# Delta rule: the inverse of each block of 14 by two blocks of 7 and one product of halves

## The chip, the cores and the metric

One core of a Trainium2 chip. The time is device microseconds (us) of one execution. The kernel before took 1900.37 us, the median of 3 runs (1899.91 to 1904.96).

## The reference, cut to what matters

A decoder of two layers for 16 sequences of 112 tokens, width 256. The diff touches the first mixer, a gated delta rule with 8 heads of 128:

```python
def step(S, inp):
    q_t, k_t, v_t, beta_t, alpha_t = inp
    S = S * alpha_t[..., None, None]
    kv = jnp.einsum('bhk,bhkv->bhv', k_t, S)
    S = S + jnp.einsum('bhk,bhv->bhkv', k_t, (v_t - kv) * beta_t[..., None])
    o_t = jnp.einsum('bhk,bhkv->bhv', q_t, S)
    return (S, o_t)
_, o = lax.scan(step, S0, (qt, kt, vt, bt, at))
```

Then a norm and a gate of o, an output product, cross attention, experts, attention, cross attention and a feed-forward part. Over all 112 tokens the recurrence is a triangular system, 112x112 for each sequence and head, which the kernel inverts in blocks: 14x14 blocks on the diagonal, pairs of them joined to 28x28, and the rest by products on TensorE.

## The kernel before, in words

**Units.** A unit is one head and four sequences (NG = 4 units to a head, 32 units). Each engine has its program written out in one order and waits on semaphores. In the main loop (lines 1022 to 1052 for DVE), unit u is solved and put out while the keys of unit u + 8 are projected. A head's inverse is made in the four units before its first solve. `head_due(u, left)` gives the head that is due in `left` units, so the units fall in four kinds by u mod 4:
- kind 0: rows 1 to 9 of the due head's blocks (`rows(h4, ...)`, in three places of the unit)
- kind 1: rows 10 and 11 ahead of the unit's key taps, rows 12 and 13 and the copy `rows_first` further on (`h3`). On SP, `exchange` stores both forms of the inverse and reads them back as pairs
- kind 2: the join of the pairs in four parts (`h2`): products 0 and 2 on POOL, sums 1 and 3 on DVE; sum 3 is the last step of DVE's unit. On SP, `joined` stores the result, as the last step of the unit
- kind 3: `spread` (SP) puts it into the big tile, ahead of the unit's `diagonal`, which stores the diagonal blocks of a new unit; `gather` reads a head's blocks into `NI`.

Head 0 is done ahead of the loop: there all 13 rows run in one piece, while PE does the first keys. Head 7 falls into the last eight units, which have a loop of their own.

**A row.** All 128 blocks of 14x14 of a head (16 sequences, 8 blocks) lie on 128 partitions, 196 values each. Row t is a product of t x t elements (L507) and a sum (L509), each waiting for the one before: row t of `NI` times the t x t corner of the inverse, summed.

**DVE's order in a unit**: key taps (L914, three instructions), the gate of unit u - 1 (`tail` 3, L976), L964, query taps, the output added to x (`tail` 5, L983), L968, then rows or the first sum of the join, the key matrix (L934), value taps (L914), rows, the z gate (L950), the query matrix (L940), L958, and rows or the second sum. Row work stands in this queue like the rest.

**PE's order in a unit** around it: key projection (L556), L645, query projection (L556), L679, L651, L589, then `tail` 4: L686, the output product, which waits for `gated` from DVE's L976. PE's transposes of the values (L616) wait for the value taps. Every period that is spoken of below runs from one L686 to the next.

**ACT and POOL.** ACT scales the output (L836), which waits for POOL's root (L1117 and L1119), and starts each tap sum (L790, L793, L804). POOL makes the masks of decay (L1092, L1104, L1112, L1113) and the products of the join (L528).

Of the kernel before, what the change touches and what calls it, by code (L numbers as in the profile page):

```python
# [12 lines left out]
ALU = mybir.AluOpType  # L13
# [72 lines left out]
def memory(nc, ctx):  # L86
# [74 lines left out]
    k.R = [p3(k.big_a[0:T, 6, :]), p3(k.big_b[0:T, 7, :])]  # L161
    at = 2 * G * DK + G * FAR
    k.A, k.A_less = four(spare[:, at:at + G * MID]), four(spare[:, at + G * MID:at + G * FAR])
    k.NI, k.TI = (k.big_a[:, 0, n * BLOCK * BLOCK:(n + 1) * BLOCK * BLOCK] for n in range(2))
    k.tri_tmp = k.big_a[:, 7, :]
    later = k.expert_w[:, :, :].rearrange("p a b -> p (a b)")
    k.Dn = [later[0:T, n * B * T:(n + 1) * B * T].rearrange("p (s t) -> p s t", s=B) for n in range(2)]
# [302 lines left out]
def is_late(u):  # L470

    return u >= UNITS - AHEAD

# [18 lines left out]
    return k.kT[n], k.qT[n]  # L492


def invert_row(dve, k, s, h, t):

    first = (2 * (BLOCK - 1) + 1) * h + 2 * (t - 1)
    if t == 1:
        dve.wait_ge(s["ni_in"], 32 * (h + 1))
        if h:  # L500
            dve.wait_ge(s["td_w"], 32 * h)
    if first:
        dve.wait_ge(s["tri"], first)
    NI = k.NI.rearrange("p (m t) -> p t m", m=BLOCK)[:, t, 0:t]
    TI = k.TI.rearrange("p (c m) -> p c m", c=BLOCK)
    tmp = k.tri_tmp[:, 0:t * t].rearrange("p (c m) -> p c m", c=t)
    dve.tensor_tensor(tmp, NI.unsqueeze(1).to_broadcast([128, t, t]), TI[:, 0:t, 0:t], ALU.mult).then_inc(s["tri"], 1)  # L507
    dve.wait_ge(s["tri"], first + 1)
    dve.tensor_reduce(TI[:, 0:t, t], tmp, AXX, ALU.add).then_inc(s["tri"], 1)  # L509


def rows_first(dve, k, s, h):

    dve.wait_ge(s["tri"], (2 * (BLOCK - 1) + 1) * (h + 1) - 1)
    dve.tensor_copy(k.TIn.rearrange("p (t c) -> p t c", t=BLOCK),
                    k.TI.rearrange("p (c t) -> p t c", c=BLOCK)).then_inc(s["tri"], 1)
# [390 lines left out]
def gdn_dve(dve, k, s):  # L907
# [77 lines left out]

    def rows(h, ts):
        for t in ts:
            invert_row(dve, k, s, h, t)

    start_dve_stats(dve, k, s, 0)  # L990
    for g in range(1, NG):
# [8 lines left out]
    for a in range(1, AHEAD + 1):  # L1000
        for slot in (2, 4, 3, 10):
            if a == 1 and slot == 10:
                start_dve_gate_in(dve, k, s, 1)
            elif a == 2 and slot == 2:
                start_dve_gate_out(dve, k, s, 1)
            elif a == NG + 1 and slot == 3:
                rows(0, range(1, BLOCK))
                rows_first(dve, k, s, 0)
            elif a == NG + 3 and slot == 4:
                for part in (1, 2, 3):  # L1010
                    join(dve, k, s, 0, part)
            elif a == NG + 4 and slot == 4:
                values(0, 7)
            if slot in (4, 10):
                keys(a - 1, slot)
            elif a < AHEAD:
                keys(a, slot)
        if a == 2:
            dve.tensor_scalar(k.norm_w[:, :], k.norm_w[:, :], 0.5, None, ALU.mult).then_inc(s["setup_dve"], 1)
    values(0, 9)  # L1020
    solve(0, "M")
    for u in range(UNITS - AHEAD):
        a = u + AHEAD
        h4, h3, h2 = head_due(u, 4), head_due(u, 3), head_due(u, 2)
        if h3 is not None:
            rows(h3, (10, 11))
        keys(a, 2)
        if u:
            tail(u - 1, 3)
        solve(u, "less")  # L1030
        keys(a, 3)
        if u:
            tail(u - 1, 5)
        solve(u, "R")
        if h4 is not None:
            rows(h4, (1, 2, 3, 4))
        if h3 is not None:
            rows(h3, (12, 13))
            rows_first(dve, k, s, h3)
        if h2 is not None:  # L1040
            join(dve, k, s, h2, 1)
        keys(a, 4)
        values(u + 1, 7)
        if h4 is not None:
            rows(h4, (5, 6))
        values(u + 1, 9)
        keys(a, 10)
        solve(u + 1, "M")
        if h4 is not None:
            rows(h4, (7, 8, 9))  # L1050
        if h2 is not None:
            join(dve, k, s, h2, 3)
    for u in range(UNITS - AHEAD, UNITS):
        more = is_unit(u + 1)
        h4, h3, h2 = head_due(u, 4), head_due(u, 3), head_due(u, 2)
        if h4 is not None:
            rows(h4, range(1, 6))
        if h3 is not None:
            rows(h3, range(11, BLOCK))
            rows_first(dve, k, s, h3)  # L1060
        if h2 is not None:
            join(dve, k, s, h2, 1)
        tail(u - 1, 3)
        solve(u, "less")
        if more:
            values(u + 1, 7)
            values(u + 1, 9)
            solve(u + 1, "M")
        else:
            cross_head_dve(dve, k, s, 0, 0)  # L1070
        solve(u, "R")
        if h4 is not None:
            rows(h4, range(6, 11))
        if h2 is not None:
            join(dve, k, s, h2, 3)
        tail(u - 1, 5)
# [90 lines left out]
def gdn_sp(sp, k, s, a):  # L1167
# [25 lines left out]
    def gather(h):  # L1193

        sp.wait_ge(s[f"nd_w{h % 2}"], 256 * (h // 2 + 1))
        if h:
            sp.wait_ge(s["tri"], (2 * (BLOCK - 1) + 1) * h)
            sp.wait_ge(s["pair"], 4 * h)
        for e, at in enumerate((FIRST, SECOND)):
            sp.dma_start(square(half(k.NI, e)), pairs(k.nd[h % 2, :, :, at, at])).then_inc(s["ni_in"], 16)  # L1200
        for e in range(2):
            sp.dma_start(square(half(k.C_full, e)), pairs(k.nd[h % 2, :, :, FIRST, SECOND])).then_inc(s["c_in"], 16)

    def exchange(h):


        sp.wait_ge(s["tri"], (2 * (BLOCK - 1) + 1) * (h + 1))
        if h >= 2:
            sp.wait_ge(s[f"dn_in{h % 2}"], 192 * (h // 2))
        for dram, tile in ((k.td, k.TI), (k.tn, k.TIn)):  # L1210
            sp.dma_start(dram[h % 2].rearrange("e s p a b -> (e s p) (a b)"), tile).then_inc(s["td_w"], 16)
        sp.wait_ge(s["td_w"], 32 * (h + 1))
        if h:
# [28 lines left out]
    for u in range(-AHEAD, UNITS):  # L1242
# [2 lines left out]
            joined(0)  # L1245
        h = head_due(u, 1) if u >= 0 else 0 if unit == NG + 3 else None
        if h is not None:
            spread(h)
        if is_unit(unit):
            if unit % NG == 0 and 1 <= unit // NG < HEADS - 1:  # L1250
# [1523 lines left out]
def sync_program(sp, k, s, a, out):  # L2774
# [170 lines left out]
```

## Time and profile before

| what | value |
|---|---|
| median of 3 runs | 1900.37 us |
| the profiled execution, its own time | 1900.15 us |
| its span | 1898.8 us |
| mean granted clock of TensorE | 0.994 |
| busy: PE, DVE, ACT, POOL | 96%, 63%, 38%, 37% |
| delta-rule stage | from the start to some 575 us |
| rows of head 0 | 61.6 to 70.0 us |
| main loop, 24 units | some 103 to 480 us |

The profile lists the instructions of each engine by line, with the time for which the engine stood idle just before them and what ended that. PE is busy nearly all of the time, so what matters in the delta-rule stage is where PE stood idle and for whom. A busy time of PE is not PE at its peak: matmuls are pipelined and their ends are modelled.

### The profile page before, as it was taken

How to read it: one execution, taken by the hardware profiler on the slowest of the kernel's cores; microseconds unless marked ns; L12 is line 12 of the kernel's file. 1: busy time of each engine (PE TensorE's matmuls, PEld its weight loads, DVE VectorE, ACT ScalarE, POOL GpSimd, SP SyncE). 2: the span in 40 equal slices, each digit the busy share in tenths (PEclk: the TensorE clock that was granted, in tenths of full speed). 3: DMA queues.
4: the chain of work that ended last, by engine and by line, in shares of the span. 5: the costliest groups of instructions: out<-in, count | busy, mean ns of one | idle time of the engine just before them, and what ended most of it. 6: DMA issues, size and time to landing. Idle time of an engine off the chain costs nothing.

```text
span 1898.8 us, 40078 instructions
## 1 busy us (share of the span) xinstructions
PE 1828.3 (96%) x15048; PEld 1324.9 (70%) x15048; DVE 1196.1 (63%) x3307; ACT 712.7 (38%) x1883; POOL 705.9 (37%) x758
## 2 busy tenths in 40 slices
PE   7799999999889999999999999999999999999999
PEld 4467777777666666666445766666659979889698
DVE  6878788778646767767766666667665334234332
ACT  4233434343435555554001465655632212122221
POOL 4644544454215766665000267666634000000000
PEclk9899999999999999999999999999999999999999
DMA  6111111111103100100000001001040000000000
GB/s 188 29 23 21 32 17 29 21 25 16 23 13 125 37 26 26 37 26 20 1 1 1 10 20 29 20 20 30 11 178 1 1 11 1 10 1 1 10 1 10
DMA packets 94591, 52.22 MB, mean 28 GB/s; under 512 B 77256, under 2 KB 86336, under 8 KB 93632
## 3 DMA queue, kind: packets, MB, share of 16 engines
q1 hardware_dynamic: 94400, 49.65, 9.8%
q8 instruction: 122, 2.00, 0.4%
q14 instruction: 69, 0.57, 0.1%
HBM read 44.18 MB, written 5.45 MB: 26 GB/s over the span
## 4 chain that ended last, share of the span: by engine, by line
PE 75%; DVE 11%; issue 6%; POOL 4%; ACT 2%; SPq 1%; DMA 1%; DVEq 0%; ACTq 0%; POOLq 0%
PE ps L2536 18%; PE ps L1519 6%; PE ps L2408 5%; PE ps L1541 5%; PE ps L2067 5%; PE ps L1596 4%; PE ps L1557 4%; PE ps L1575 4%; PE ps L556 3%; PE ps L2614 3%; DVE big_b L914 3%; PE ps L686 2%; DVE big_a L507 2%; PE ps L1528 2%; PE ps L1662 2%
## 5 line engine op out<-in xcount | busy, mean ns | idle before, releaser
L1980 POOL TENSOR_TENSOR h_w<-h_w 125x336 int32<-125x336 int32 x384 | 336.3, 906 | 210.6 <-ACT h_w L1761 210.4
L1865 DVE CUSTOM_DVE_ANT_0 h_w<-ps,h_w 112x375 f32<-112x375 f32 x512 | 263.1, 543 | 0.5 <-PE ps L1519 0.2
L914 DVE SCALAR_TENSOR_TENSOR big_b<-ps,taps,big_b 128x444 f32<-128x444 f32 (+2 forms) x288 | 193.9, 673 | 67.7 <-ACT big_b L790 49.6
L1761 ACT ACTIVATE h_w<-ps 125x336 f32<-125x336 f32 x512 | 198.0, 468 | 21.6 <-PE ps L1541 21.6
L272 POOL TENSOR_TENSOR rstd<-var_eps,minus_half 112x4 f32<-112x4 f32 x12 | 12.2, 1018 | 406.5 <-DVE var_eps L259 406.5
L1541 PEld LDWEIGHTS ps<-h_w 32*125 32x125 f32 x3072 | 96.0, 183 | 62.0 <-issue 61.2
L1541 PE MATMUL ps<-h_w 32*125 32x112 f32 x3072 | 118.0, 282 | 7.7 <-DVE h_w L1865 5.0
L1874 DVE TENSOR_TENSOR h_w<-h_w,ps 128x112 f32<-128x112 f32 x128 | 34.7, 271 | 141.7 <-PE ps L1528 141.5
L1519 PE MATMUL ps<-h_w 32*112 32x375 f32 x1024 | 121.2, 519 | 0.8 <-DVE h_w L1865 0.8
L2067 PE MATMUL ps<-expert_w,big_a 128*112 128x512 f32 x256 | 113.6, 595 | 0.0
L556 PE MATMUL ps<-h_w,w 128*128 128x448 f32 x256 | 108.2, 545 | 4.7 <-ACT h_w L812 4.7
L556 PE MATMUL ps<-h_w,kq_w 128*128 128x448 f32 x256 | 111.3, 558 | 0.0
L1557 PE MATMUL ps<-h_w 125*32 125x112 f32 x3072 | 100.8, 263 | 0.5 <-POOL h_w L1980 0.4
L2408 PE MATMUL ps<-xT,w 128*128 128x448 f32 x256 | 97.7, 540 | 1.1 <-DVE big_a L2423 1.1
L2178 DVE SCALAR_TENSOR_TENSOR x<-ps,small,x 112x256 f32<-112x256 f32 x128 | 61.9, 483 | 37.0 <-PE ps L2067 34.0
L2067 PEld LDWEIGHTS ps<-expert_w,big_a 128*112 128x112 f32 x256 | 43.9, 177 | 57.5 <-issue 48.0
L1884 DVE TENSOR_TENSOR h_w<-h_w 125x336 f32<-125x336 f32 x128 | 81.7, 638 | 2.5 <-ACT h_w L1761 2.4
L2408 PEld LDWEIGHTS ps<-xT,w 128*128 128x128 f32 x256 | 48.3, 190 | 46.6 <-issue 44.8
L1557 PEld LDWEIGHTS ps<-h_w 125*32 125x32 f32 x3072 | 69.9, 109 | 15.6 <-issue 1.2
L1112 POOL TENSOR_TENSOR big_a<-big_a,w 112x448 f32<-112x448 f32 x32 | 31.3, 980 | 131.3 <-ACT big_a L798 112.1
L2536 PE MATMUL ps<-big_b,h_w 128*128 128x224 f32 x384 | 79.0, 353 | 0.0
L2536 PE MATMUL ps<-big_a,h_w 128*128 128x224 f32 x384 | 78.5, 352 | 0.0
(357 smaller groups left out, 3848.4 us busy)
## 6 DMA issues: line engine op xcount, KB each, us to landing
h_w<-in_h SPq DMA_DIRECT2D x2, 4096.0 KB, 16.9
kq_w<-in_ctxT SPq DMA_DIRECT2D x16, 375.0 KB, 3.1
h_w<-in_ctxT SPq DMA_DIRECT2D x16, 375.0 KB, 3.2
h_w<-in_mask SPq DMA_DIRECT2D x16, 164.1 KB, 3.1
kq_w<-in_kq_w SPq DMA_DIRECT2D x8, 256.0 KB, 3.4
w<-in_vz_w SPq DMA_DIRECT2D x8, 256.0 KB, 3.5
blocks<-h_w SPq DMA_DIRECT2D x128, 12.2 KB
expert_w<-in_expert_w SPq DMA_DIRECT2D x1, 2048.0 KB
```

The lines of the kernel that those rows point to most:

```text
L556: ins = pe.matmul(ps[:, bank, 0:GT], w[:, c, :], c_in[:, c, :], start=(c == 0), stop=(c == KD - 1))
L914: dve.scalar_tensor_tensor(p3(dst)[:, :, i:], p3(ps[:, bank, 0:GT])[:, :, 0:T - i], k.taps[:, h, n, TAPS - 1 - i:TAPS - i], p3(dst)[:, :, ...
L1519: pe.matmul(ps[0:T, score_bank(Q, r), 0:S2], k.Qz[n % 2][rows, z, m, :], k.Kx[n % 2][rows, z, m, :], start=True, stop=True).then_inc(s["S" ...
L1541: ins = pe.matmul(ps[0:CK, turned_bank(Q, r), c * T:(c + 1) * T], k.Kx[n % 2][rows, z, m, c * CK:(c + 1) * CK], k.Qx[Q % 2][rows, :], star ...
L1557: ins = pe.matmul(ps[32 * r:32 * r + 32, 6, q * T:(q + 1) * T], k.Vx[n % 2][:, c, 4 * q + r, :], k.PTx[(4 * Q + r) % RING][:, c * T:(c + 1 ...
L1761: act.activation(k.PTx[(4 * Q + r) % RING], ps[0:CK, turned_bank(Q, r), 0:NC * T], ACT.Exp).then_inc(s["exp"], 1)
L1865: dve.tensor_tensor_reduce(k.masked[r % 2], ps[0:T, score_bank(Q, r), 0:S2], k.mask_add[n % 2], -1.0, 3.0e38, ALU.add, ALU.min, k.neg_max[ ...
L1884: dve.tensor_tensor(P, P, k.mask_I[n % 2], ALU.min).then_inc(s["weights0"], 1)
L1980: pool.tensor_tensor(P.bitcast(I32), P.bitcast(I32), k.mask_I[n % 2], ALU.mult).then_inc(s["weights"], 1)
L2067: ins = pe.matmul(ps[0:T, bank, :], k.moe_xT[g % 2][:, c, j * T:(j + 1) * T], k.expert_w[:, c, e * D:(e + 2) * D], start=(c == 0), stop=(c ...
L2408: ins = pe.matmul(k.ps[:, 2 + 2 * n + m % 2, 0:GT], k.w12[:, n, c, m * 128:(m + 1) * 128], k.xT[:, c, :], start=(c == 0), stop=(c == KD - 1))
L2536: ins = pe.matmul(ps[:, product_bank(p, m), FIRST_HALF], lhsT, rhs, start=(c == 0), stop=(c == QT - 1))
```

## The change

Each 14x14 block is cut in two blocks of 7 on its diagonal and a 7x7 block between them. Rows 1 to 6 of both small blocks are made in the same instructions (`invert_half_row`; row 1 is a copy), then the block between by two products with a sum each (`join_halves`, parts 0 and 1, 343 elements each). Both tiles get a row's width more room so that a view reaches both halves. Where row 7 and further stood, the parts of `join_halves` stand. The second sum of the pairs' join goes from the end of unit kind 2 to the start of the next, and `joined` on SP with it; in the last eight units neither is moved.

```diff
+SMALL_DONE = 2 * HALF + 2
...
-    k.NI, k.TI = (k.big_a[:, 0, n * BLOCK * BLOCK:(n + 1) * BLOCK * BLOCK] for n in range(2))
+    wide = BLOCK * (BLOCK + 1)
+    k.NI, k.TI = (k.big_a[:, 0, n * wide:(n + 1) * wide] for n in range(2))
...
-def invert_row(dve, k, s, h, t):
-
-    first = (2 * (BLOCK - 1) + 1) * h + 2 * (t - 1)
+def halves_of(block):
+
+    return block.rearrange("p (e r) -> p e r", e=2)[:, :, 0:HALF * BLOCK].rearrange("p e (c m) -> p e c m", m=BLOCK)[:, :, :, 0:HALF]
+
+
+def invert_half_row(dve, k, s, h, t):
+
+    first = SMALL_DONE * h + (2 * t - 3 if t > 1 else 0)
+    N, inverse = halves_of(k.NI), halves_of(k.TI)
     if t == 1:
         dve.wait_ge(s["ni_in"], 32 * (h + 1))
         if h:
             dve.wait_ge(s["td_w"], 32 * h)
-    if first:
+            dve.wait_ge(s["tri"], first)
+        dve.tensor_copy(inverse[:, :, 0, 1], N[:, :, 0, 1]).then_inc(s["tri"], 1)
+    else:
         dve.wait_ge(s["tri"], first)
-    NI = k.NI.rearrange("p (m t) -> p t m", m=BLOCK)[:, t, 0:t]
-    TI = k.TI.rearrange("p (c m) -> p c m", c=BLOCK)
-    tmp = k.tri_tmp[:, 0:t * t].rearrange("p (c m) -> p c m", c=t)
-    dve.tensor_tensor(tmp, NI.unsqueeze(1).to_broadcast([128, t, t]), TI[:, 0:t, 0:t], ALU.mult).then_inc(s["tri"], 1)
+        tmp = k.tri_tmp[:, 0:2 * t * t].rearrange("p (e c m) -> p e c m", e=2, c=t)
+        dve.tensor_tensor(tmp, N[:, :, 0:t, t].unsqueeze(2).to_broadcast([128, 2, t, t]), inverse[:, :, 0:t, 0:t],
+                          ALU.mult).then_inc(s["tri"], 1)
+        dve.wait_ge(s["tri"], first + 1)
+        dve.tensor_reduce(inverse[:, :, 0:t, t], tmp, AXX, ALU.add).then_inc(s["tri"], 1)
+
+
+def join_halves(dve, k, s, h, part):
+
+    first = SMALL_DONE * h + 2 * HALF - 3 + 2 * part
+    N = k.NI[:, 0:BLOCK * BLOCK].rearrange("p (m t) -> p t m", m=BLOCK)
+    inverse = k.TI[:, 0:BLOCK * BLOCK].rearrange("p (c m) -> p c m", c=BLOCK)
+    shape = [128, HALF, HALF, HALF]
+    tmp = k.tri_tmp[:, 0:HALF ** 3].rearrange("p (c a b) -> p c a b", c=HALF, a=HALF)
+    between = k.tri_tmp[:, HALF ** 3:HALF ** 3 + HALF * HALF].rearrange("p (c a) -> p c a", c=HALF)
+    if part == 0:
+        rows, cols, to = inverse[:, 0:HALF, 0:HALF], N[:, HALF:, 0:HALF], between
+    else:
+        rows, cols, to = between, inverse[:, HALF:, HALF:].rearrange("p n t -> p t n"), inverse[:, 0:HALF, HALF:]
+    dve.wait_ge(s["tri"], first)
+    dve.tensor_tensor(tmp, rows.unsqueeze(2).to_broadcast(shape), cols.unsqueeze(1).to_broadcast(shape), ALU.mult).then_inc(s["tri"], 1)
     dve.wait_ge(s["tri"], first + 1)
-    dve.tensor_reduce(TI[:, 0:t, t], tmp, AXX, ALU.add).then_inc(s["tri"], 1)
+    dve.tensor_reduce(to, tmp, AXX, ALU.add).then_inc(s["tri"], 1)
...
     def rows(h, ts):
         for t in ts:
-            invert_row(dve, k, s, h, t)
+            if t < HALF:
+                invert_half_row(dve, k, s, h, t)
+            else:
+                join_halves(dve, k, s, h, t - HALF)
...
-                rows(0, range(1, BLOCK))
+                rows(0, range(1, HALF + 2))
                 rows_first(dve, k, s, 0)
...
-        h4, h3, h2 = head_due(u, 4), head_due(u, 3), head_due(u, 2)
+        h4, h3, h2, h1 = head_due(u, 4), head_due(u, 3), head_due(u, 2), head_due(u, 1)
+        if h1:
+            join(dve, k, s, h1, 3)
         if h3 is not None:
-            rows(h3, (10, 11))
+            rows(h3, (7,))
         keys(a, 2)
...
         solve(u, "R")
         if h4 is not None:
-            rows(h4, (1, 2, 3, 4))
+            rows(h4, (1, 2, 3))
         if h3 is not None:
-            rows(h3, (12, 13))
+            rows(h3, (8,))
             rows_first(dve, k, s, h3)
         if h2 is not None:
             join(dve, k, s, h2, 1)
         keys(a, 4)
         values(u + 1, 7)
         if h4 is not None:
-            rows(h4, (5, 6))
+            rows(h4, (4,))
         values(u + 1, 9)
         keys(a, 10)
         solve(u + 1, "M")
         if h4 is not None:
-            rows(h4, (7, 8, 9))
-        if h2 is not None:
-            join(dve, k, s, h2, 3)
+            rows(h4, (5, 6))
     for u in range(UNITS - AHEAD, UNITS):
...
-            rows(h4, range(1, 6))
+            rows(h4, range(1, 4))
         if h3 is not None:
-            rows(h3, range(11, BLOCK))
+            rows(h3, range(7, HALF + 2))
             rows_first(dve, k, s, h3)
...
-            rows(h4, range(6, 11))
+            rows(h4, range(4, 7))
...
         h = head_due(u, 1) if u >= 0 else 0 if unit == NG + 3 else None
         if h is not None:
+            if h and not is_late(u):
+                joined(h)
             spread(h)
...
         h = head_due(u, 2) if u >= 0 else None
-        if h is not None:
+        if h is not None and is_late(u):
             joined(h)
```

The counts of the semaphore `tri` and the DMAs of `NI` and `TI` follow: 16 steps a head where there were 27, and the first 196 values of each wider tile.

## Rows read from the trace of the kernel before

**Rows 1.** The page: busy time, share and instructions of each engine.
```profile
PE 1828.3 (96%) x15048; PEld 1324.9 (70%) x15048; DVE 1196.1 (63%) x3307; ACT 712.7 (38%) x1883; POOL 705.9 (37%) x758
```

**Rows 2.** Busy time by stretch: length, PE, PEld, DVE, ACT, POOL, clock, DMA share, GB/s.
```profile
182.90:246.35 63.45, 61.84 (x416) 45.58 (x416) 52.15 (x102) 25.69 (x80) 29.99 (x31) 1.00 0.14 24
...
373.20:438.30 65.10, 63.52 (x417) 46.49 (x417) 52.27 (x103) 25.68 (x80) 30.02 (x31) 0.97 0.14 20
```

**Rows 3.** Timeline of PE: start, us, line, tiles [idle before, its releaser].
```profile
214.09 1.98 PE L686 MATMUL ps<-gdn_out_w,big_b 128*112 128x256 f32 x8 [0.36 <-DVE big_b L976]
...
229.47 1.89 PE L686 MATMUL ps<-gdn_out_w,big_b 128*112 128x256 f32 x8
...
240.84 0.83 PE L645 MATMUL ps<-big_b,h_w 112*84 112x84 f32 x8
...
246.35 1.98 PE L686 MATMUL ps<-gdn_out_w,big_b 128*112 128x256 f32 x8 [1.23 <-DVE big_b L976]
...
261.72 1.89 PE L686 MATMUL ps<-gdn_out_w,big_b 128*112 128x256 f32 x8
```

**Rows 4.** Timeline of DVE in unit kind 0 and the start of kind 2.
```profile
233.01 0.38 DVE L507 TENSOR_TENSOR big_a<-big_a 128x1 f32<-128x1 f32 x1
...
233.61 0.67 DVE L507 TENSOR_TENSOR big_a<-big_a 128x4 f32<-128x4 f32 x1
...
235.30 0.62 DVE L934 TENSOR_TENSOR h_w<-ps,big_a 112x448 f32<-112x448 f32 x1
...
237.85 0.78 DVE L507 TENSOR_TENSOR big_a<-big_a 128x25 f32<-128x25 f32 x1
...
239.23 0.61 DVE L950 SCALAR_TENSOR_TENSOR big_b<-big_b,ps 128x448 f32<-128x448 f32 x1
...
240.71 0.22 DVE L507 TENSOR_TENSOR big_a<-big_a 128x49 f32<-128x49 f32 x1
...
243.62 2.09 DVE L914 SCALAR_TENSOR_TENSOR big_b<-ps,taps,big_b 128x444 f32<-128x444 f32 x3
...
258.56 2.10 DVE L914 SCALAR_TENSOR_TENSOR big_b<-ps,taps,big_b 128x444 f32<-128x444 f32 x3 [2.61 <-ACT big_b L790]
```

**Rows 5.** Groups of DVE by shape: count, busy us, mean ns of one, idle before.
```profile
L507 DVE TENSOR_TENSOR big_a<-big_a 128x169 f32<-128x169 f32 x8 | 3.6, 447 | 0.3
...
L509 DVE TENSOR_REDUCE big_a<-big_a 128x13 f32<-128x169 f32 x8 | 2.6, 330 | 0.3
...
L528 DVE TENSOR_TENSOR w<-w 128x1372 f32<-128x1372 f32 x1 | 2.0, 1957 | 0.0
...
L507 DVE TENSOR_TENSOR big_a<-big_a 128x49 f32<-128x49 f32 x8 | 1.8, 230 | 0.1
```

**Rows 6.** Timeline of POOL in unit kind 0.
```profile
233.33 0.94 POOL L1104 TENSOR_TENSOR big_a<-upto,small 112x448 f32<-112x448 f32 x1
...
236.64 1.04 POOL L1119 TENSOR_TENSOR rstd<-var_eps,minus_half 112x4 f32<-112x4 f32 x1
237.65 0.94 POOL L1092 TENSOR_TENSOR soft<-before,small 112x448 f32<-112x448 f32 x1
```

**Rows 7.** Head 0: DVE's row 4 and copy, PE behind them, busy time by stretch.
```profile
63.73 0.18 DVE L507 TENSOR_TENSOR big_a<-big_a 128x16 f32<-128x16 f32 x1
...
69.71 0.33 DVE L515 COPY w<-big_a 128x196 f32<-128x196 f32 x1
...
72.10 1.84 PE L594 MATMUL ps<-big_b 128*112 128x112 f32 x8 [5.37 <-DVE big_b L914]
...
72.10:76.40 4.30, 4.30 (x12) 2.98 (x13) 2.95 (x5) 0.55 (x1) 3.65 (x4) 0.50 0.20 42
```

**Rows 8.** Timeline of PE in head 5.
```profile
373.19 3.57 PE L686 MATMUL ps<-gdn_out_w,big_b 128*112 128x256 f32 x8 [1.23 <-DVE big_b L976]
```

**Rows 9.** Head 7: timelines of POOL and PE.
```profile
501.10 2.89 POOL L528 TENSOR_TENSOR w<-w 128x1372 f32<-128x1372 f32 x1 [7.63 <-issue]
...
506.65 0.60 PE L679 MATMUL ps<-ident,xn 112*128 112x112 f32 x4 [0.88 <-ACT xn L836]
```

More of the change, by code:

```diff
@@ L508, in invert_row @@
     dve.wait_ge(s["tri"], first + 1)
-    dve.tensor_reduce(TI[:, 0:t, t], tmp, AXX, ALU.add).then_inc(s["tri"], 1)
+    dve.tensor_reduce(to, tmp, AXX, ALU.add).then_inc(s["tri"], 1)
 def rows_first(dve, k, s, h):
-    dve.wait_ge(s["tri"], (2 * (BLOCK - 1) + 1) * (h + 1) - 1)
+    dve.wait_ge(s["tri"], SMALL_DONE * (h + 1) - 1)
     dve.tensor_copy(k.TIn.rearrange("p (t c) -> p t c", t=BLOCK),
-                    k.TI.rearrange("p (c t) -> p t c", c=BLOCK)).then_inc(s["tri"], 1)
+                    k.TI[:, 0:BLOCK * BLOCK].rearrange("p (c t) -> p t c", c=BLOCK)).then_inc(s["tri"], 1)
@@ L1196, in gather @@
         if h:
-            sp.wait_ge(s["tri"], (2 * (BLOCK - 1) + 1) * h)
+            sp.wait_ge(s["tri"], SMALL_DONE * h)
             sp.wait_ge(s["pair"], 4 * h)
         for e, at in enumerate((FIRST, SECOND)):
-            sp.dma_start(square(half(k.NI, e)), pairs(k.nd[h % 2, :, :, at, at])).then_inc(s["ni_in"], 16)
+            sp.dma_start(square(half(k.NI[:, 0:BLOCK * BLOCK], e)), pairs(k.nd[h % 2, :, :, at, at])).then_inc(s["ni_in"], 16)
         for e in range(2):
@@ L1204, in exchange @@
     def exchange(h):
-        sp.wait_ge(s["tri"], (2 * (BLOCK - 1) + 1) * (h + 1))
+        sp.wait_ge(s["tri"], SMALL_DONE * (h + 1))
         if h >= 2:
             sp.wait_ge(s[f"dn_in{h % 2}"], 192 * (h // 2))
-        for dram, tile in ((k.td, k.TI), (k.tn, k.TIn)):
+        for dram, tile in ((k.td, k.TI[:, 0:BLOCK * BLOCK]), (k.tn, k.TIn)):
             sp.dma_start(dram[h % 2].rearrange("e s p a b -> (e s p) (a b)"), tile).then_inc(s["td_w"], 16)
@@ L2789, in sync_program @@
                        (k.minus_strict[:, :], "minus_strict"), (k.norm_w[:, :], "norm_w"),
-                       (k.off_blocks[:, :], "off_blocks"), (k.TI, "block_eye")):
+                       (k.off_blocks[:, :], "off_blocks"), (k.TI[:, 0:BLOCK * BLOCK], "block_eye")):
         sp.dma_start(tile, a[name]).then_inc(s["c_gdn"], 16)
```

## Prediction

> **What bounds the kernel now.** I read the page first: PE is busy 96% of the span and DVE 63% [rows 1]. That is an average over stages, and the diff touches only the delta-rule stage, so I cut the trace by heads. One head's four units take 63.45 us, of which PE is busy 61.84 [rows 2]: the stage runs at PE's pace, less some idle time. The timeline of PE shows whose it is. The output matmuls of L686 stand once in each unit, in a fixed place of PE's order, so their starts are a clock: 214.09, 229.47, 246.35, 261.72 [rows 3]. Three of a head's four periods are 15.4 to 15.8; that of kind 0 (the unit that does most rows) is 246.35 - 229.47 = 16.88. It holds a 1.23 wait for DVE's L976, a slip of 0.14 at L645 (the 112x84 matmuls start at 240.84 and take 0.83) and a first matmul after idling that makes L686 1.98 instead of 1.89. A period without a stall is 261.72 - 246.35 = 15.37. So DVE costs 16.88 - 15.37 = 1.51 us a head here. The same wait of 1.23 or 1.24 stands ahead of L686 in six heads (units 1, 5, 9, ... 21). A second, smaller one (0.36 at 214.09, kind 3) has another cause: POOL runs both of the join's products in unit kind 2, its root comes late, and ACT's scaling and tap behind it.
>
> In DVE's timeline of that period [rows 4] the reader is to see that DVE does not wait once: rows 1 to 4 from 233.01, rows 5 and 6 from 237.85, rows 7 to 11 from 240.71, and only at 243.62 the key taps, behind which L976 stands. In the next unit, where DVE waits for ACT's tap, they start at 258.56, 3.16 ahead of L686. Without the stall L686 would stand at 229.47 + 15.37 = 244.84, and the taps would be ready at 241.7. The row work is on the path.
>
> **The second sum: nothing.** The join's part 3 was the last thing that DVE did in unit kind 2 and becomes the first in kind 3. Nothing stands between the two places. On SP, `joined` was the last step of kind 2 and now comes just ahead of `spread` in kind 3: again the same order, before the same four diagonal stores. In the last eight units neither moves. Queue for queue the instructions are in the same order, so I cost it at 0; it has one answer.
>
> **The inversion, in instructions.** Before, a head has 13 products, 13 sums and a copy (27 instructions, 819 products of elements). After, it has a copy, 5 pairs over both halves (2t² elements, 180 in all), 2 pairs of 343 elements and the old copy: 16 instructions, 866 elements. The elements stay; 11 instructions go, with some 0.15 us fixed and 0.03 between two.
>
> The prices are from the groups by shape [rows 5]. A product of 49 elements takes 230 ns and one of 169 takes 447, of which 150 is the floor of one element: 1.6 to 1.8 ns an element. The only product of DVE with 98 short rows of operands in a row, 1372 elements, takes 1957: 1.32 ns an element. For 343 that gives 0.60 to 0.75 us. I take 0.75, since its second operand is read with a stride of 14, as in the rows of today. Sums are 330 for 169 elements, 1.04 ns each over a floor of 0.155: 0.51 for 343. A half join is then 0.75 + 0.51 + 0.07 = 1.33. The pairs of both halves come to 0.17 + 0.16, 0.18 + 0.17, 0.20 + 0.19, 0.24 + 0.21 and 0.27 + 0.23 for t = 2 to 6.
>
> The Trainium skill (VectorE: DVE Perf Modes, the section on the TRN2 errata) states (N + 151)/0.96 ns for an fp32 tensor_tensor. An estimate from that page is 515 ns for N = 343; it also gives 333 for N = 169 where the trace has 447, so the trace decides. With the page's price a half join would be 0.24 cheaper and the sum below about 0.5 us larger.
>
> **Contention between DVE and POOL.** Two products take far longer than their shape: 4 elements, 0.67, from 233.61, and 25 elements, 0.78, from 237.85 [rows 4]. They end at 234.28 and 238.63, just as POOL's L1104 (233.33 + 0.94) and L1092 (237.65 + 0.94) end [rows 6]. A DVE product with both inputs in SBUF stands while POOL runs such an operation; sums do not. The Trainium skill (SBUF — State Buffer, the section that has the exclusive lock of the shared port pair) says the same and adds that the one that starts first holds it for its whole instruction. By that rule a product that comes ahead of POOL's operation is free and one just behind waits it out, which makes this term two-valued here.
>
> **Walk through kind 0 of a head.** Row 1 and the products of row 2 still stand behind POOL until 234.28. Then the sum of row 2 and row 3 end at 234.9 instead of 235.30: 0.4 gained (0.8 if the copy slips through). L934 and the three value taps take 2.55, so row 4 comes at 237.43. There POOL's root (L1119, 236.64 + 1.04) is running, not yet L1092. Bounds: the product gets in between the two, at 237.7, and the pair ends at 237.95; or it stands until 238.6 and ends at 238.85. L950 started at 239.23, so DVE is then 1.38 or 0.46 ahead. Its last stretch took 243.62 - 240.71 = 2.91. Now it is rows 5 and 6 (0.24 + 0.21 + 0.27 + 0.23 + 0.14 = 1.09) and half a join (1.29), 2.4 with rounding: 0.5 gained. The key taps start 1.9 or 1.0 earlier than 243.62, at 241.7 or 242.6. PE can reach L686 at 244.84 and starts it 2.73 after those taps start (246.35 - 243.62): they must start by 242.1. So the stall is gone, or 0.5 of it is left. The gain per head is 1.5 or 1.0. I take 1.4, nearer to the first since row 4 meets the boundary between two POOL operations, where the product at 233.01 was let through. What is late next is PE itself; ACT's tap allows 241.7.
>
> Six heads: 6 x 1.4 = 8.4. In unit 0 the value taps are also late for PE's transposes (0.30, L616), and 0.4 earlier they are not: 0.3.
>
> **Kind 1.** Rows 12 and 13 with the copy took 1.87 ahead of L934 at 251.86; half a join and the copy take 1.7. PE does not wait for DVE there now. SP's stores, the exchange and POOL's first product come some 0.3 earlier relative to PE; they gain nothing, since POOL's second product stands behind DVE's sum, and that sum behind L968. So 0, and the 0.36 of kind 3 stays.
>
> **Head 0.** Its rows run in one piece, and PE stands for it (5.37 us before 72.10 [rows 7]). The first three rows again meet POOL and keep their times. From row 4 at 63.73 to the copy at 69.71 it is 5.98; after, rows 4 to 6 take 0.39 + 0.45 + 0.50 + 0.2 = 1.5 and the two half joins 2.7: 4.2. Gain 1.8, all of it on the path, since the exchange, POOL's first product and the taps behind it all shift. After the idle time PE ran at a granted clock of 0.50, its 1.2 GHz level, for 4.3 us [rows 7]; it would now start at 70.3, and I take it that the clock falls all the same, since 3.6 us of idle time are left. Ends: 1.5, and 3.6 if it doesn't fall, as 4.3 us at half speed are some 2 us too many.
>
> **The clock in head 5.** In one of the six stalls L686 took 3.57 instead of 1.98 [rows 8]; the mean granted clock of that head is 0.97 where it is 1.00 in the other, and it took 65.10 [rows 2]. PE had stood idle for 1.23 just before. Without that idle time I expect it to go: 1.6. Ends: 0 and 1.6.
>
> **Head 7**, in the last eight units. DVE mostly waits there, so shorter rows are hidden. One chain counts: rows, exchange, POOL's product at 501.10, which holds POOL's root until 504.07, and PE's L679 waits 0.88 for ACT behind it [rows 9]. The rows end 0.8 earlier; the root is then held by its squares. Gain 0.5 (0.3 to 0.6).
>
> **Sum.** 8.4 + 0.3 + 1.8 + 1.6 + 0.5 = 12.6 us. The profiled execution took 1900.15 (span 1898.8 and 1.35 around it), 0.2 from the median of 1900.37. 1900.15 - 12.6 = 1887.5.
>
> **Rivals.**
> 1. POOL holds the ports. Row 4 stands until 238.6 in each head, and the clock still dips once. 6 x 1.0 + 0.3 + 1.8 + 0.5 = 8.6, 1891.5. For it: 0.67 and 0.78 in the rows. Against: row 4 would come while L1119 runs, ahead of L1092. Chance 0.22.
> 2. The clock gives more. Head 0's matmuls keep or regain full speed, 6 x 1.5 + 0.3 + 3.6 + 1.6 + 0.5 = 15.0, 1885.1. Against: 3.6 us of idle time are three times the 1.23 at which it fell once in six. Chance 0.18.
> 3. The wide products are slow. The stage returns little: with two broadcast operands in four dimensions each costs 1.6 us (4.7 ns an element), the last stretch of kind 0 then takes 3.2, 0.3 more than the 2.91 of today, against 0.46 to 1.38 that row 4 brings. 6 x 0.6 and 0.5 for head 7 are 4.1, 1896. No row is above 1.8 ns on DVE. Chance 0.08.
> 4. Slower. The same mechanism further: if a product of 343 costs more than 1.8 to 2.7 us, the key taps start later than 243.62, PE's wait grows by the excess in each of six heads, and head 0 loses twice the excess. At 3.5 us that is 6 x 1.2 + 3.7 = 11 slower, 1911. It would take over 8 ns an element. Chance 0.04.
>
> That the change does not do what it says holds for its second half, costed at 0, and moves no number.
>
> **How the numbers follow.** The forecast, stall gone, dip gone, head 0 by DVE's time, has 0.48. The range reaches to rivals 1 and 2 and their ends: rival 2 with products of 0.60 is 1884; rival 1 with head 0 at 1.5 and head 7 at 0.3 is 1892.0, which I round up to 1893 since the clock is priced from single events. I give 1883.5 to 1893. A measurement of this kernel tells about 0.3% (5.7 us) from no change. Forecast and rivals 1 and 2 are faster by more: 0.88. Rival 3 is within: 0.08. Rival 4: 0.04.
>
> **What would show it.** After: L686 in the timeline of PE every 15.4 also in kind 0, with a wait for L976 under 0.4; DVE idle before the key taps of kind 1, released by ACT L790; 343-element products of 0.6 to 0.75 and sums of 0.51; row work of head 0 in 6.6 instead of 8.4; the same 0.36 in kind 3; and the join's sum in the same place. What would make it wrong: the wide product's price, where row 4 falls against POOL's L1092, and the clock.

## The result, and the profile after

The kernel with the change takes 1885.78 us (median of 4 runs, 1884.67 to 1886.9); the kernel before takes 1900.14 (1897.98 to 1904.96). The ratio is 0.9921, 95% interval 0.9901 to 0.9941: 0.8% faster, with 1887.5 forecast and a range of 1883.5 to 1893.0. The profiled execution took 1886.9, the slowest of the four, with a span of 1885.5; before it was 1898.8. So the two traces differ by 13.3 us, where the medians differ by 14.4, and it is the 13.3 that have to be found.

The page of after first, then the first head's cut that [rows 2] made of before (length, busy time of PE, PEld, DVE, ACT and POOL, granted clock, DMA share, GB/s):

```profile
PE 1823.0 (97%) x15048; PEld 1324.1 (70%) x15048; DVE 1183.2 (63%) x3219; ACT 712.2 (38%) x1883; POOL 709.5 (38%) x758
...
177.44:239.15 61.71, 61.38 (x418) 45.58 (x417) 50.59 (x91) 25.64 (x80) 30.46 (x30) 1.00 0.15 25
```

DVE has 88 instructions and 12.9 us fewer, 11 a head. The head takes 61.71 where it took 63.45, while PE's busy time in it fell by only 0.46: the rest, 1.28, was PE standing idle. POOL's busy time rose by 3.6 us over the span; it has the same 758 instructions, so some of them take longer. Nearly all of it is the second mask of L1134 in kind 1, which takes 1.46 where it takes 0.93 elsewhere (the mean of its group is 1087 ns for 978), beside DVE's second wide product.

The timeline of PE in the same head (start, length, line, tiles; L713 is what L686 was):

```profile
223.87 1.89 PE L713 MATMUL ps<-gdn_out_w,big_b 128*112 128x256 f32 x8
...
235.11 0.76 PE L672 MATMUL ps<-big_b,h_w 112*84 112x84 f32 x8
...
239.15 1.89 PE L713 MATMUL ps<-gdn_out_w,big_b 128*112 128x256 f32 x8
...
254.43 1.89 PE L713 MATMUL ps<-gdn_out_w,big_b 128*112 128x256 f32 x8
...
270.20 1.98 PE L713 MATMUL ps<-gdn_out_w,big_b 128*112 128x256 f32 x8 [0.33 <-DVE big_b L1003]
```

Against [rows 3]: the period of kind 0 is 239.15 - 223.87 = 15.28, with no wait and no slip at the 112x84 matmuls (0.76 for 0.83); the next is 15.28 too; only the small wait of kind 3 is left (0.33 for 0.36).

The timeline of DVE in that period, which answers to [rows 4], and of POOL, which answers to [rows 6]:

```profile
227.42 0.38 DVE L511 COPY big_a<-big_a 128x2 f32<-128x2 f32 x1
227.83 0.86 DVE L515 TENSOR_TENSOR big_a<-big_a 128x8 f32<-128x8 f32 x1
...
229.31 0.62 DVE L961 TENSOR_TENSOR h_w<-ps,big_a 112x448 f32<-112x448 f32 x1
...
231.86 0.20 DVE L515 TENSOR_TENSOR big_a<-big_a 128x32 f32<-128x32 f32 x1
...
234.75 0.77 DVE L534 TENSOR_TENSOR big_a<-big_a 128x343 f32<-128x343 f32 x1
235.55 0.51 DVE L536 TENSOR_REDUCE big_a<-big_a 128x49 f32<-128x343 f32 x1
235.99 2.10 DVE L941 SCALAR_TENSOR_TENSOR big_b<-ps,taps,big_b 128x444 f32<-128x444 f32 x3
```

```profile
227.73 0.93 POOL L1134 TENSOR_TENSOR big_a<-upto,small 112x448 f32<-112x448 f32 x1
...
231.04 1.04 POOL L1149 TENSOR_TENSOR rstd<-var_eps,minus_half 112x4 f32<-112x4 f32 x1
232.05 0.93 POOL L1122 TENSOR_TENSOR soft<-before,small 112x448 f32<-112x448 f32 x1
```

The key taps start 239.15 - 235.99 = 3.16 ahead of L713; before it was 2.73, which was too little. Row 2's product (8 elements, 0.86) still stands until POOL's L1134 ends, at 228.7. But row 4's product, on which the forecast turned, runs at 231.86 in 0.20, in the last fifth of POOL's root L1149 (231.04 to 232.08) and just ahead of L1122. It is so in five of the six kinds 0. In the first one (unit 0) DVE and POOL stand a little differently, and the product comes just behind the start of L1122 and waits it out:

```profile
108.00 0.93 POOL L1122 TENSOR_TENSOR soft<-before,small 112x448 f32<-112x448 f32 x1
```

```profile
108.14 0.84 DVE L515 TENSOR_TENSOR big_a<-big_a 128x32 f32<-128x32 f32 x1
```

### Where the 13.3 us went

The start of the same output matmuls in the kernel before (those of [rows 3] and [rows 8] are not repeated). Rows with fewer than 8 matmuls come from a narrow window that cut them off; only their starts are read:

```profile
119.50 1.76 PE L686 MATMUL ps<-gdn_out_w,big_b 128*112 128x256 f32 x7 [1.24 <-DVE big_b L976]
182.92 1.33 PE L686 MATMUL ps<-gdn_out_w,big_b 128*112 128x256 f32 x5 [1.24 <-DVE big_b L976]
309.76 1.55 PE L686 MATMUL ps<-gdn_out_w,big_b 128*112 128x256 f32 x6 [1.23 <-DVE big_b L976]
438.24 1.98 PE L686 MATMUL ps<-gdn_out_w,big_b 128*112 128x256 f32 x8 [1.23 <-DVE big_b L976]
```

and in after:

```profile
115.63 1.55 PE L713 MATMUL ps<-gdn_out_w,big_b 128*112 128x256 f32 x6 [0.38 <-DVE big_b L1003]
177.44 1.89 PE L713 MATMUL ps<-gdn_out_w,big_b 128*112 128x256 f32 x8
300.85 1.46 PE L713 MATMUL ps<-gdn_out_w,big_b 128*112 128x256 f32 x6
363.05 1.25 PE L713 MATMUL ps<-gdn_out_w,big_b 128*112 128x256 f32 x5
424.75 1.46 PE L713 MATMUL ps<-gdn_out_w,big_b 128*112 128x256 f32 x6
```

Before minus after is 3.87, 5.48, 7.20 (at 246.35 [rows 3]), 8.91, 10.14 (at 373.19 [rows 8]) and 13.49. From head to head it grows by 1.61, 1.72, 1.71, 1.23 and 3.35: 1.6 to 1.7 for each head's kind 0, with two exceptions. In the head that gained 1.23, after has a longer stall of its own in kind 3 (0.82 at 332.40; POOL's first product of the join came 1.6 later there than in the head before, relative to PE): 0.5 lost. In the head that gained 3.35 the slow clock of [rows 8] is gone: 1.6. Of the first 3.87, 2.16 are there by PE's query projection of unit 0 (100.63 before, 98.47 after), which is head 0; the other 1.71 is unit 0's kind 0: 0.47 up to the transposes, 0.38 at the 112x84 matmuls and 0.86 of the wait, which is 0.38 where it was 1.24. Behind the last of these another 0.1 comes from the period after that stall, next to nothing from head 7 (there a gain and a loss of 0.6 cancel, below), and 0.3 is lost in the rest of the program, which is not touched.

| term | forecast | measured |
|---|---|---|
| kind 0 of unit 0, with its value taps | 1.4 + 0.3 | 1.7 |
| kind 0, the other five | 7.0 | 8.6 |
| head 0 | 1.8 | 2.2 |
| slow clock in head 5 | 1.6 | 1.6 |
| head 7 | 0.5 | 0.0 |
| second sum moved | 0 | 0 (a run of its own, below) |
| later stall at 332.40, rest of the program | 0 | -0.8 |
| sum | 12.6 | 13.3 |

### The profile page after: what moved, and what is told of

It is laid out like the page before. It is cut to its first block, busy times and chain, and to the rows that moved or that the text cites. A ratio compares the mean times of both kernels' runs of the same rounds, so it can differ in the third digit from the quotient of the medians.

```text
span 1885.5 us, 39990 instructions
## 1 busy us (share of the span) xinstructions
PE 1823.0 (97%) x15048; PEld 1324.1 (70%) x15048; DVE 1183.2 (63%) x3219; ACT 712.2 (38%) x1883; POOL 709.5 (38%) x758
## 4 chain that ended last, share of the span: by engine, by line
PE 80%; DVE 7%; issue 6%; POOL 4%; ACT 2%; SPq 1%; DMA 1%; DVEq 0%; ACTq 0%; POOLq 0%
PE ps L2568 18%; PE ps L1551 6%; PE ps L2440 5%; PE ps L1573 5%; PE ps L2099 5%; PE ps L583 5%; PE ps L1628 4%; PE ps L1589 4%; PE ps L1607 4%; PE ps L2646 3%; PE ps L713 2%; PE ps L1560 2%; PE ps L1694 2%; PE ps L1639 1%; DVE big_b L941 1%
```

## The experiments

Theory A is the forecast's: DVE's row work is on the path in kind 0 and head 0, and the time is in the instructions taken out. The rivals that had to be told apart: the moved sum brings part of it (B); the slack is not at kind 0, so that row work anywhere costs the same (C); the clock and not the work sets the size (D). All experiments but one (the root edit on the kernel before) start from the kernel with the change; the times are medians, and each ratio is against the kernel before on the same chip, whose median was 1899.69 to 1901.35 there. So times of different runs are compared to within 1 or 2 us, and finer readings are taken from the traces.

### The inversion alone

```diff
-        if h1:
-            join(dve, k, s, h1, 3)
...
+        if h2 is not None:
+            join(dve, k, s, h2, 3)
```

with `joined` back at the end of SP's unit.

> The changed kernel with the join's second sum and its stores back in their old places in the program. My theory: these places hold the same order on each queue, so the time is that of the changed kernel, 1884.5 to 1887, and the page shows the same waits. Rival: the move carries part of the gain (the sum no longer stands in unit kind 2), and without it the kernel is 2 us or more slower.

Measured: 1885.34 us (1885.17 to 1885.76), ratio 0.9926 (0.9911 to 0.9941), span 1884.4. The move is worth 0.4 us the wrong way, inside the spread of either: B falls, and the term of 0 stands. Its L713 stand 15.28, 15.37 or 15.77 apart just as in after.

### The row work put back, by place

The first sum of a half join (0.51, 0.54 with its wait) is done five times in place of once, in one place at a time; its result is the same.

```diff
+    if part == 0 and 1 <= h <= 6:
+        for i in range(4):
+            dve.tensor_reduce(to, tmp, AXX, ALU.add).then_inc(s["extra"], 1)
+            dve.wait_ge(s["extra"], 4 * (h - 1) + i + 1)
```

Kind 0 of heads 1 to 6 as above:

> The changed kernel with the first sum of the block between done five times instead of once in the main loop (heads 1 to 6), in unit kind 0 just ahead of the key taps: four more sums of 0.54 us, 2.16 a head, with nothing else moved. My theory: DVE's work there is on the path once some 0.4 us of slack is used up, so a head costs 2.16 - 0.4 and the slower first matmuls after idling, 1.8 to 1.9: 6 heads, 11 us slower than the changed kernel, about 1897, with a wait of some 1.7 ahead of the output product L713's place in unit kind 1. Rival: the gain came from the clock or another queue and DVE is hidden there: under 2 us.

Measured: 1899.84 us (1897.99 to 1907.25), ratio 1.0004 (0.9991 to 1.0016): the whole gain is gone. The timeline of PE has the stall back in every head, 1.57 for the 1.23 of before (2.55 in unit 1):

```profile
245.64 1.98 PE L717 MATMUL ps<-gdn_out_w,big_b 128*112 128x256 f32 x8 [1.57 <-DVE big_b L1007]
```

Some 2.2 us of sums went in. A head's kind 0 and the period behind it rose by 1.8 together in five heads (17.02 and 15.37 for 15.28 twice; before minus after has 1.7 in it) and unit 1's L717 stands 2.6 later than in the inversion alone. The cost against the inversion alone is 14.5 and not 11: 5 x 1.8 + 2.6 make 11.7, and the clock fell behind two of the six waits (L717 takes 3.51 and 3.67 instead of 1.98), 1.6 each: 14.9 up to unit 22's L717, and 14.2 over the span.

Kind 1 (`part == 1`, heads 1 to 6), where I had counted row work as free:

> The changed kernel with four more sums (2.16 us a head) in unit kind 1, just ahead of the copy, for heads 1 to 6. My theory: there DVE has slack, but not 2.16: the value taps come 2.16 later and PE's transposes wait some 0.7, and the exchange and POOL's first product come as much later, which costs some 0.7 in kind 3. 0.7 to 1.4 a head, 4 to 8 us, 1890 to 1894. Rival a: all hidden, under 1 us. Rival b: as on the path as in kind 0, 11 us.

Measured: 1892.6 us (1890.89 to 1897.03), ratio 0.9962 (0.9952 to 0.9972), 6.8 slower than after. The same 2.2 us cost 1.1 a head here, and 2.4 a head with the clock in kind 0. PE now waits ahead of its transposes of the values in this unit:

```profile
250.66 0.65 PE L647 MATMUL ps<-ident,big_b 128*112 128x128 f32 x4 [0.75 <-DVE big_b L945]
```

Head 0 (`part == 0 and h == 0`):

> The changed kernel with four more sums of 0.54 us (2.16) in the row work of head 0 alone. My theory: that work is on the path one for one, also for the exchange and POOL behind it, so 2.0 to 2.4 slower, about 1887.7. Rival: DVE later waits for something else (the 2.4 us for ACT's tap) and takes it up: under 0.7.

Measured: 1889.8 us (1888.07 to 1890.85), ratio 0.9943 (0.9927 to 0.9959), 4.0 slower than after. PE's wait for the rows is 5.80 (3.62 in the kernel it is nearest to, the inversion alone):

```profile
72.26 1.84 PE L625 MATMUL ps<-big_b 128*112 128x112 f32 x8 [5.80 <-DVE big_b L945]
```

So 2.2 us of DVE's work come back one for one. The rest, which I had not expected, is more time at the clock's lower level further on: the granted clock from 76 to 100 us is 0.71 for 0.79, and unit 1's L717 stands 3.4 later than in the inversion alone. C falls: the same instructions cost 2.2 and 1.2 of clock in head 0, 1.1 in kind 1, 1.8 to 2.6 and sometimes a dip in kind 0.

### The last small stall

Kind 3's 0.33 was put down to POOL's late root. In unit kind 2 POOL makes two masks (L1134) for the next unit, which nobody awaits yet, ahead of the root; here the root goes first.

```diff
+        if h2 is not None:
+            root(u)
         if is_unit(u + AHEAD + 1):
             fades(u + AHEAD + 1)
-        root(u)
+        if h2 is None:
+            root(u)
```

> The changed kernel with POOL's root of the output norm ahead of its two fade masks in unit kind 2, instead of behind them. My theory of the 0.33 us stall in unit kind 3: POOL runs the join's second product, then the fades, then the root, and ACT's scaling and key tap wait for it. The root comes 1.9 us earlier, so the stall goes in 6 heads: 0.5 a head, 3 us faster, 1882 to 1883.5, and also the one stall of 0.82. Rival: the root then waits for ACT's squares and holds up the masks behind it, which DVE needs: same or slower.

Measured: 1882.61 us (1882.08 to 1884.6), ratio 0.9913 (0.9898 to 0.9929), 3.2 faster than after, and 2.7 faster than the inversion alone on the same chip. The timelines of POOL and PE:

```profile
257.78 2.88 POOL L555 TENSOR_TENSOR w<-w 128x1372 f32<-128x1372 f32 x1 [1.13 <-DVE w L567]
260.75 0.23 POOL L1147 TENSOR_SCALAR var_eps<-var_eps 112x4 f32<-112x4 f32 x1
261.06 1.04 POOL L1149 TENSOR_TENSOR rstd<-var_eps,minus_half 112x4 f32<-112x4 f32 x1
```

```profile
252.58 1.89 PE L713 MATMUL ps<-gdn_out_w,big_b 128*112 128x256 f32 x8
...
267.86 1.89 PE L713 MATMUL ps<-gdn_out_w,big_b 128*112 128x256 f32 x8
```

Every period of the main loop from unit 2 on is now 15.28, and no L713 waits; only unit 1's 0.38 stays. In after kind 3's period is 270.20 - 254.43 = 15.77, 0.49 more, and the next 0.09 more; six of them make 3.5. The same edit on the kernel before:

> The kernel before with POOL's root ahead of the masks in unit kind 2, and nothing else. Theory: the 0.36 us stall of kind 3 is POOL's own and has nothing to do with the inversion, so it goes here as well, 0.5 a head in 6 heads: 1896.5 to 1897, with the 1.23 waits of kind 1 as before. Rival: with DVE late in kind 1 the root is not what the unit waits for, and nothing changes.

Measured: 1896.59 us (1894.15 to 1897.6), ratio 0.9975 (0.9965 to 0.9985), 4.8 below the 1901.35 beside it, with an interval of 2.9 to 6.7. It keeps kind 0's stall (the wait ahead of L686 at 245.46 is 1.24). Its six heads gain 3.5 in the trace by the small stall. It also had no slow clock in head 5, another 1.6 there, but one near 885 us (0.66 from 885 to 890) that before lacks, so the clock's part of the 4.8 is open. Kind 3's stall, then, was there before, had another cause, and the change did not touch it.

### The clock in head 0

PE stands idle twice for DVE there (4.23 and 6.40 in after), and runs at 0.50 of the full clock behind each. Filler matmuls on PE in those gaps, into a bank that nobody reads, should keep the clock:

```diff
+            if slot == 10 and a in (NG + 2, AHEAD):
+                for _ in range(9 if a < AHEAD else 14):
+                    pe.matmul(ps[:, 5, 0:GT], k.ident[:, :], k.gdn_xT[:, 0, 0], start=True, stop=True)
```

> The changed kernel with 9 and 14 matmuls of 448 columns, into a bank that nobody reads, at the two places of the first head where PE stands idle for DVE (4.2 and 6.4 us). They leave nothing out. My theory: the idle time lowers the granted clock, and matmuls at half speed behind it are on the path; with PE busy the clock stays up and the kernel is 3 to 5 us faster, about 1882. Rival: PE at half speed is hidden by DVE there, and the time is the same within 1 us.

Measured: 1885.68 us (1884.35 to 1886.05), ratio 0.9926 (0.9912 to 0.9941): nothing gained. The timeline of PE says why:

```profile
66.19 6.94 PE L750 MATMUL ps<-h_w,ident 128*128 128x448 f32 x18
...
81.71 10.70 PE L750 MATMUL ps<-h_w,ident 128*128 128x448 f32 x28
```

Nine calls are 18 records of 0.38, so the fillers were twice as long as I had reckoned, and ended after the taps that PE was to wait for. The clock stayed at 1.00, and the gain went into the overrun. With 5 and 8 calls:

> As the filler run, with 5 and 8 matmuls in place of 9 and 14. In the longer one each took 0.38 us twice, so the fillers ran for 6.9 and 10.7 us, over the idle times of 4.2 and 6.4, and held PE back by 2 to 3 us at either place while the clock stayed at 1.00; it gained nothing. Theory: these two effects cancelled. 5 and 8 take 3.8 and 6.1 us and end before DVE does, so the gain of the full clock is left: 2 to 4 us faster than the changed kernel, 1881.5 to 1883.5. Rival: half speed behind the idle time is hidden, 1885 to 1886 again.

Measured: 1885.55 us (1883.6 to 1886.34), ratio 0.992 (0.9905 to 0.9936). Also nothing, for another reason: the clock held through both gaps and fell behind a third, short one, where the 112x84 matmuls take 1.76 instead of 0.93.

```profile
88.02 0.65 PE L643 MATMUL ps<-ident,big_b 128*112 128x128 f32 x4 [1.50 <-DVE big_b L944]
89.32 1.76 PE L658 MATMUL ps<-expert_w,h_w 112*112 112x84 f32 x8 [0.66 <-DMA expert_w<-joined]
```

L713 of unit 1 stood 1.3 earlier than in the inversion alone (113.22 for 114.48). Two dips of the clock stand later in the program, near 550 and 1380 us; the inversion alone has only the first, so the second took that back. By itself this run decides nothing on D. So the last one closes the third gap too, with two more calls ahead of unit 0's value transposes, and takes the root first:

> The changed kernel with both edits: POOL's root ahead of the masks in unit kind 2, and fillers of 5, 8 and 2 matmuls in the first head (the last two in the 1.5 us that PE still stood for the value taps, after which the clock had fallen to 0.5 at about 88 us in the shorter filler run). Nothing is left out. Theory: the root gives 3.0 as alone, the clock of the first head some 2.5 (its first output product came at 113.22 against 114.48 with only part of the slow stretch gone): 1880 to 1881.5. Rival: single dips of the clock later on (about 550 and 1380 us, 1.6 us each) take the second part back, 1882.5.

Measured: **1877.5 us (1877.1 to 1878.4), ratio 0.9875 (0.9857 to 0.9893)**, span 1876.4, mean granted clock 0.999: 8.3 faster than after, 5.1 faster than with the root alone (by the ratios, each against its own chip's kernel before, 8.7 and 7.2). Busy time by stretch, for after and for this kernel (columns as above):

```profile
60.00:76.00 16.00, 11.77 (x45) 7.42 (x44) 11.54 (x26) 3.61 (x7) 7.86 (x9) 0.80 0.27 38
76.00:100.00 24.00, 16.69 (x83) 12.23 (x82) 17.67 (x24) 4.25 (x8) 13.12 (x11) 0.78 0.30 45
```

```profile
60.00:76.00 16.00, 15.81 (x72) 9.48 (x71) 14.20 (x29) 4.58 (x8) 8.44 (x10) 1.00 0.21 33
76.00:100.00 24.00, 23.08 (x128) 14.63 (x129) 20.17 (x31) 4.92 (x9) 14.68 (x13) 1.00 0.32 46
```

Its timeline of PE shows that the fillers end just ahead of the real work, which waits 0.18 and 0.24 for its taps, and where unit 1's output matmuls stand: 110.48, for 114.48 in the inversion alone and 114.96 in the kernel with the root alone.

```profile
75.87 1.04 PE L621 MATMUL ps<-big_b 128*112 128x112 f32 x8 [0.18 <-DVE big_b L946]
...
79.28 6.19 PE L750 MATMUL ps<-h_w,ident 128*128 128x448 f32 x16
85.71 1.04 PE L621 MATMUL ps<-big_b 128*112 128x112 f32 x8 [0.24 <-DVE big_b L946]
...
110.48 1.98 PE L713 MATMUL ps<-gdn_out_w,big_b 128*112 128x256 f32 x8 [0.37 <-DVE big_b L1008]
```

So the clock in head 0 was worth another 4.0 to 4.5 us, some twice what the shorter rows brought there. This bears on D: the clock explains what was left in head 0, not what the change brought in kind 0, where PE ran at 1.00 in all heads but one.

### Head 7

The forecast had 0.5 here, and in sum nothing of it came. The period that held the wait of 0.88 [rows 9] did get shorter, 11.37 for 11.95, and that wait is 0.29. But the period before it got as much longer, 12.00 for 11.45. It is that of unit 25, which in after has this (timelines of DVE, POOL and PE):

```profile
478.47 0.76 DVE L534 TENSOR_TENSOR big_a<-big_a 128x343 f32<-128x343 f32 x1
...
478.47 0.85 POOL L1147 TENSOR_SCALAR var_eps<-var_eps 112x4 f32<-112x4 f32 x1 [14.36 <-ACT xn L856]
...
481.67 0.60 PE L706 MATMUL ps<-ident,xn 112*128 112x112 f32 x4 [0.92 <-ACT xn L863]
```

The wide product and the first step of POOL's root start together, and the latter takes 0.85 where it takes 0.23 elsewhere. Here all of head 7's row work is done in the unit before:

```diff
-        if h3 is not None:
-            rows(h3, range(7, HALF + 2))
-            rows_first(dve, k, s, h3)
...
-            rows(h4, range(4, 7))
+            rows(h4, range(4, HALF + 2))
+            rows_first(dve, k, s, h4)
```

> The changed kernel with all of head 7's rows, both half joins and the copy in unit 24 (its first of the last eight), none in unit 25. Theory of why head 7 brought 0.1 and not 0.5: in unit 25 DVE's second wide product (478.47, 0.76 us) ran when POOL's root was due and held it for 0.62, so PE waited 0.92 for ACT where it had waited 0.37. With the products earlier POOL's L1147 takes 0.23 and not 0.85, and PE's waits there are 0.3 to 0.4: 0.5 us faster, seen in the trace and hardly in the time. Rival: the wait stays 0.9, as the squares are late themselves.

Measured: 1886.09 us (1885.02 to 1886.95), ratio 0.9924 (0.9909 to 0.994), which can't be told from after. In the trace the cause is plain:

```profile
478.53 0.23 POOL L1145 TENSOR_SCALAR var_eps<-var_eps 112x4 f32<-112x4 f32 x1 [14.36 <-ACT xn L856]
...
481.26 0.60 PE L706 MATMUL ps<-ident,xn 112*128 112x112 f32 x4 [0.45 <-ACT xn L863]
```

With the product gone from beside it the root's step is short, PE waits 0.45 instead of 0.92, and the period is 11.53 instead of 12.00. So the cause is shown. The 0.5 doesn't show in the time: this trace has a dip of the clock near 550 us (1.6) that after's lacks.

## Why the prediction was right, and where it was off

**What bounds the stage.** Right. DVE work put back into kind 0 brought back the stall (1.57 for 1.23) and the whole time.

**The wide operations.** Forecast 0.75 and 0.51. The groups of DVE by shape:

```profile
L534 DVE TENSOR_TENSOR big_a<-big_a 128x343 f32<-128x343 f32 x16 | 13.2, 825 | 0.3
L536 DVE TENSOR_REDUCE big_a<-big_a 128x49 f32<-128x343 f32 x16 | 8.2, 510 | 0.6
```

The product is 0.74 to 0.77 where it is alone, as extrapolated from the 447 of [rows 5]; the mean of 825 has kind 1 in it (0.97, beside POOL's L1134). An estimate from the Trainium skill's (N + 151)/0.96 (VectorE: DVE Perf Modes, the section on the TRN2 errata) is 515 ns for 343 elements; the shortest record here is 741, so the measurement decides. Rival 3 needed 1.6 us, rival 4 over 1.8: both are excluded.

**Row 4 and POOL.** The forecast took 1.4 a head, between 1.0 (held by L1122) and 1.5 (not held), and both ends occurred: unit 0 has the held one and keeps 0.38 of its stall, for which the forecast had 0.5; the other five have the free one. Rival 1 is what happened once in six. The reasoning was off in one point: the product does not slip through between two POOL operations, it runs while the root's L1149 is under way on its four columns. The rule that I drew on (the Trainium skill, SBUF — State Buffer, the section "SBUF: two separate sides", where the one that starts first holds the lock for its whole instruction) is borne out by row 2 (0.86 beside L1134, 0.17 alone in head 0), by row 4 in unit 0 (0.84) and by POOL's L1147 (0.85 instead of 0.23 beside DVE's product), and not by row 4 beside L1149 (0.20).

**The size of a kind 0.** The mis-sized term: 8.6 for five, forecast 7.0. I took the undisturbed period as 261.72 - 246.35 = 15.37 [rows 3]. That period begins with the L686 that restarts after the stall and takes 1.98 instead of 1.89. The undisturbed one is 15.28. A head's stall cost 16.88 - 15.28 = 1.60, and 0.09 in the next period: 1.7. The forecast took 1.4 of its 1.51: 0.1 of the 0.3 that a head is off is that hedge for row 4, and 0.2 is the base. A period that begins inside the disturbance is no base for its price. Before's main loop has no period that neither follows nor holds a wait, but the correction stood in [rows 3]: 15.37 less the 0.09 by which the restarting L686 is longer (1.98 - 1.89) is 15.28. The root edit on the kernel before, which has such periods, shows it (213.29 - 198.01 = 15.28).

**Head 0.** 2.2 for 1.8, by three errors. From the first row to the taps it is 68.79 - 62.81 = 5.98; before, the taps started at 69.96 and row 1 at 61.60, 8.36: 2.4 less. I had let the first three rows keep their times since POOL holds them; here only the copy is held (0.65), which is the 0.6 more. Against that stands a transfer ahead of the rows, in the chain of waits of after (start, length, what), with the first row and the matmuls behind the exchange in the timelines:

```profile
56.25 2.99 DMA blocks<-h_w
```

```profile
62.81 0.65 DVE L511 COPY big_a<-big_a 128x2 f32<-128x2 f32 x1 [1.75 <-DMA big_a<-blocks]
```

```profile
88.78 1.84 PE L621 MATMUL ps<-big_b 128*112 128x112 f32 x8 [6.40 <-DVE big_b L941]
```

The transfer took 1.46 in before's, so the rows began 1.2 later in this execution, and 1.0 of gain was left at the next matmuls that wait for the exchange (88.78 for 89.80). It is this one execution: in the ten others whose chain shows the transfer, eight of them with the change, it took 1.44 to 1.46. In the inversion alone those matmuls start at 87.56 and unit 1's L713 at 114.48 instead of 115.63. Over the five kernels with the change whose program is the same up to there, that matmul stands at 114.48 to 115.66, so the 2.2 of head 0 is one sample of 2.2 to 3.3. The last part is the clock, which I had counted as 0: PE is back at speed by 97.9, before by 100.6, and the 1.0 becomes 2.16. So the total of head 0 is near the forecast partly by luck: 0.6 and 1.1 more came than was in the term, and 1.2 less by the transfer.

**The clock in head 5.** 1.6 came as forecast, in this pair. But over the runs such a dip comes and goes. Near 550 us, behind PE's wait of 1.5 for ACT, eight of the nine kernels of the experiments that have the change show one, and after and the two kernels without the change do not. So this term is one event of 1.6 us, and that it came out to the tenth is luck: had after's profiled execution had the dip that eight of the nine have, the traces would show 0 for the clock outside head 0. It is right only to say that the stall gave it more occasions: one dip in six waits of 1.23 in before (none in the six that the root edit left there), two in the six longer ones of the first experiment on kind 0.

**Head 7 and kind 3.** Head 7 gave nothing instead of 0.5; the step that failed was "the root is then held by its squares": the 0.6 that was gained behind POOL's product was lost one period before, where DVE's wide product of unit 25 held the root's first step and made a new wait (0.92 for 0.37). Kind 3 stayed, as said.

## What to carry to other kernels

In a chain of small operations count the instructions and not the elements (here 88 fewer instructions on about as many elements took 12.9 us off DVE's busy time, 0.15 each), and look for where in the schedule the chain runs: the same 2.2 us cost 1.1 in one unit, 1.8 in another, and more than themselves where PE's clock fell behind them. When a queue has something that is awaited and something that is not yet, put the awaited first (the root before the masks, 3 us for two lines). Filler matmuls paid for the clock when they ended before the real work and every gap was closed: with fillers that overran, the whole gain was lost, and with one gap open 1.3 of the 4.0 us came, too little to be measured in the time.

## What the runs showed of the hardware that I had not expected

- A two-input product of DVE stands beside a POOL operation on 448 columns (8 elements: 0.86 for 0.17), and a POOL operation beside a wide DVE product (4 columns: 0.85 for 0.23); a copy of 2 elements stands too (0.38 to 1.07 for 0.16). POOL's L1149 on 4 columns, 1.04 long, does not hold DVE's product that comes 0.8 into it (0.20). Why it is different was not tried.
- The granted clock fell to 0.50, the 1.2 GHz level, behind idle times of 3.6 to 7.0 us each time, and behind 1.2 to 1.6 us in some executions and not in others.
- One call of an fp32 matmul with 448 columns is two records of 0.38 us.
- The last of the diagonal blocks' stores of head 0 landed in 1.44 to 1.46 us in ten executions and in 2.99 in one, with the same instructions ahead of it.
